# Alternating the two heads of a tile in the mixer's value matmuls

## The reference

```python
x = x + _L0_attn_ref(_L0_cond_ref(x, f, f, w, u, cond), W_in, conv_w, ...)
# in _L0_attn_ref:
def step(h, inp):
    dA_t, dt_t, x_t, B_t, C_t = inp
    u = (dt_t[:, :, None] * x_t)[..., None] * B_t[:, :, None, :]
    h = dA_t[:, :, None, None] * h + u
    y = jnp.einsum('bhpn,bhn->bhp', h, C_t)
    return (h, y)
y = moveaxis(ys) + D_param[None, None, :, None] * xs
g = y * _silu(gate)
g = g * rsqrt(mean(g * g) + EPS) * norm_w
return jnp.einsum('bli,di->bld', g, W_out)
```

## Time and profile before

| | us |
|---|---|
| median of 3 runs | 1449.42 |
| lowest and highest run | 1442.3, 1452.4 |
| span of the profiled execution | 1444.4 |
| PE busy | 1208.4 (84%) |
| PE weight loads busy | 641.6 (44%) |
| DVE busy | 879.5 (61%) |
| ACT busy | 593.9 (41%) |
| POOL busy | 569.6 (39%) |
| L655 MATMUL py, 512 records, busy | 71.1 |
| DVE's y (L935) waiting for PE's py (L655) | 49.7 in 20 waits |

### The profile page before, as it was taken

How to read it: one execution, slowest core, us unless ns; L and a number is a source line. 1 busy time by engine, 2 the same in 40 slices (tenths; PEclk the granted TensorE clock), 3 DMA queues, 4 the chain that set the end, 5 groups by cost and what they waited for, 6 DMA issues and landing times. The chain is left out here.

```text
span 1444.4 us, 16409 instructions
## 1 busy us (share of the span) xinstructions
PE 1208.4 (84%) x4614; PEld 641.6 (44%) x4614; DVE 879.5 (61%) x1244; ACT 593.9 (41%) x1742; POOL 569.6 (39%) x531
## 2 busy tenths in 40 slices
PE   0048899779897699999986898988799787997998
PEld 0014444334453344444434555643485336844443
DVE  7978999389985564246325948729741496504222
ACT  2025454454454232232224546647672476711110
POOL 5562675626665231002002856727651275500000
PEclk9999999999999799999998999989899898997999
DMA  6000000000003400000003000030000000000000
GB/s 253 0 22 1 0 1 1 1 0 0 0 0 120 157 0 1 0 0 0 33 10 136 1 1 0 0 138 1 1 2 1 1 0 0 0 0 8 0 0 29
DMA packets 5481, 33.24 MB, mean 23 GB/s; under 512 B 528, under 2 KB 1936, under 8 KB 3536
## 3 DMA queue, kind: packets, MB, share of 16 engines
q1 hardware_dynamic: 5424, 32.61, 5.8%
HBM read 31.56 MB, written 1.05 MB: 23 GB/s over the span
## 5 line engine op out<-in xcount | busy, mean ns | idle before, releaser
L813 POOL TENSOR_TENSOR decays<-decays,scores 128x768 f32<-128x768 f32 x64 | 124.8, 1953 | 152.0 <-ACT decays L749 152.0
L575 PE MATMUL pg<-h,weights 128*128 (+1 forms) x136 | 66.5, 612 | 85.5 <-PEq L356 82.6
L1998 POOL TENSOR_TENSOR f_pair<-m,weights 128x256 f32<-128x256 f32 x80 | 90.9, 1156 | 92.6 <-DVE m L2019 91.6
L1101 PE MATMUL ph<-h,weights 128*128 x256 | 116.5, 600 | 0.0
L1406 POOL TENSOR_TENSOR prob_latent<-prob_latent,inverse_latent 128x128 f32<-128x128 f32 (+1 forms) x128 | 81.5, 660 | 70.4 <-DVE inverse_latent L1396 70.1
L575 PE MATMUL px<-h,weights 128*128 x136 | 73.3, 664 | 26.1 <-DVE conv L886 26.0
L749 ACT ACTIVATE decays<-pcum,neg_cum 128x256 f32<-128x256 f32 (+1 forms) x256 | 87.7, 449 | 11.4 <-PE pcum L628 11.2
L1246 DVE TENSOR_TENSOR mid<-up,ph 128x512 f32<-128x512 f32 x44 | 30.2, 687 | 98.5 <-ACT up L1158 98.5
L1406 POOL TENSOR_TENSOR prob_gqa<-prob_gqa,inverse_gqa 128x128 f32<-128x128 f32 (+1 forms) x128 | 62.0, 506 | 58.4 <-DVE inverse_gqa L1396 56.8
L1158 ACT ACTIVATE up<-ph 128x512 f32<-128x512 f32 x44 | 26.3, 597 | 140.4 <-PE ph L1101 140.4
L886 DVE SCALAR_TENSOR_TENSOR conv<-px,pp,conv 128x510 f32<-128x510 f32 (+2 forms) x102 | 75.1, 737 | 14.5 <-ACT conv L714 11.6
(11 more groups left out here) (327 smaller groups left out, 3069.6 us busy)
## 6 DMA issues: line engine op xcount, KB each, us to landing
weights<-in_w_mixer SPq DMA_DIRECT2D x2, 2048.0 KB, 18.3
weights<-in_w_moe SPq DMA_DIRECT2D x2, 1536.0 KB, 7.8
moe_rest<-in_w_moe SPq DMA_DIRECT2D x2, 1536.0 KB, 13.9
weights<-in_w_gqa SPq DMA_DIRECT2D x1, 3072.0 KB, 10.2
weights<-in_w_gqa SPq DMA_DIRECT2D x1, 2048.0 KB, 14.7
weights<-in_w_moe SPq DMA_DIRECT2D x1, 1920.0 KB, 9.1
weights<-in_w_mixer SPq DMA_DIRECT2D x1, 1536.0 KB, 11.8
weights<-in_w_moe SPq DMA_DIRECT2D x1, 1152.0 KB, 11.7
```

What stands on the lines that cost most here:

```text
L575: op = nc.tensor.matmul(out[0:m, :], w[:, col + k * m:col + (k + 1) * m], net.h[:, ds(i * PAIR + k * TOK, TOK)], start=(k == 0), stop=(k = ...
L813: nc.gpsimd.tensor_tensor(decays[:, head % 4], decays[:, head % 4], scores[:], ALU.mult).then_inc(decay_scaled, 1)
L1101: op = nc.tensor.matmul(out[:], wt[:, n * D + k * P:n * D + (k + 1) * P], net.h[:, ds(i * PAIR + k * TOK, TOK)], start=(k == 0), stop=(k = ...
L1998: op = nc.gpsimd.tensor_tensor(out[:, :, s, :], src[:, :, 1 - s, :], sin[:, None, s, :].to_broadcast([P, 4, HALF]), ALU.mult)
```

## The change

In `mix`, the loop over the two heads of the tile goes from the outside to the inside. Before, the four matmuls of the first head stood ahead of the four of the second, with a wait for `decay_scaled` ahead of each head. Now each matmul of the first head is followed by the same one of the second head, and one wait for the scaled decays of both heads stands ahead of all.

```diff
-                for hh in range(TILE_HEADS):
-                    head = s * TILE_HEADS + hh
-                    pe.wait_ge(decay_scaled, i * HEADS + head + 1)
-                    rows = slice(hh * HEAD, (hh + 1) * HEAD)
-                    for b in range(BB):
-                        for r in range(ST):
-                            cols = slice(0, SEQ) if r == 0 else slice(SEQ, TRI)
+                pe.wait_ge(decay_scaled, i * HEADS + (s + 1) * TILE_HEADS)
+                for b in range(BB):
+                    for r in range(ST):
+                        cols = slice(0, SEQ) if r == 0 else slice(SEQ, TRI)
+                        for hh in range(TILE_HEADS):
+                            head = s * TILE_HEADS + hh
+                            rows = slice(hh * HEAD, (hh + 1) * HEAD)
                             op = nc.tensor.matmul(
                                 py[rows, b * SEQ + r * P:(b + 1) * SEQ],
                                 x_tok[:, s % 3, b * ST + r, rows],
```

## The result

The changed kernel takes 1438.08 us (median of 13 runs, 1431.1 to 1450.59) against 1447.5 us for the kernel before, timed beside it (median of 13, 1442.3 to 1459.14). The ratio is 0.9933 with a 95% interval of 0.991 to 0.9955, so 6.5 to 13.0 us less, 9.7 by the ratio.

A forecast was written before the change was run, and what follows sets the result against it. Steady steps were bound by PE and a nearly equal loop through POOL's pass and DVE's gate. Terms of 0.6, 1.88, 2.04 and 1.95 made 6.5 us a pair, 13.0 for both, less 0.5: 12.5 us, so 1437 us, range 1429 to 1447.

The forecast's parts named there:

- The mix: Value matmuls: head 2 starts 0.05 us behind head 1, a mix takes 1.57, saving 0.65 (bounds 0.56 and 0.70).
- Rival C: Value matmuls: alternating heads never run at once, a mix takes 2.9 us, 17 us slower in all, 1466; chance 0.08.
- The wait costs nothing: Before the mix: waiting for both heads' scaled decays costs nothing, with 0.91 us to spare in the closest case.
- Mix 0: First mix of a pair: y's 2.33 us wait loses 0.65, g is freed, `xs` meets the pass; 0.6 counted.
- Mix 5, 1.88: Gate at 186.31 moves 0.65 earlier, ahead of POOL's pass, and takes 0.68 us: gain 1.88 us a pair.
- rival D: PE's longer waits drop its clock to 1.2 GHz, two or three times: 5 us back, 1442; 0.20 shared with another rival.
- Mix 11, 2.04: Gate at 244.03 moves ahead of POOL's pass and ends at 244.06 in place of 246.10: gain 2.04 us.
- Mixes 7 to 10: Steady steps: gate still behind POOL's pass absorbs the 0.65, PE idles for ACT's exponentials; nothing counted.
- The tie of -0.03: Steady steps: gate starts 0.62 us behind POOL and moves 0.65 earlier, so which goes first is open.
- rival B: Gate wins the tie at mix 8, 9 or 10, DVE 1.05 us earlier: 3 to 7 us more, 1430 to 1434; chance 0.20.
- The tail, 1.95: Mixes 13 to 15, where the mix is on the only chain: 3 x 0.65 = 1.95 us a pair.
- the signs named in advance: Mix 1.5 to 1.65 us, y waits about 37, gates near 186 and 244 about 0.7, mixer 12 to 13 shorter.

The follow-up runs named there:

- the kernel by batch: Against the changed kernel: for each batch the two matmuls of head 1, then the two of head 2; 1430.03 us (one run).
- second execution of before: The kernel before, unchanged, timed and profiled once more; 1454.08 us, beside 1448.17 in the run next to it.
- the kernel with the clock kept up there: Changed kernel plus two matmuls adding zeros behind mix 4 of each pair, nowhere else; 1446.1 us (one run).
- the two kernels that kept the clock up there: Changed kernel plus zero-adding matmuls: two a pair behind mix 4 only, 1446.1 us; ten a pair in PE's long waits, 1436.28 us.
- the short pass: Changed kernel with POOL's scaling cut from 768 to 16 columns, so the output differs; 1408.49 us (one run), 1421.38 for the kernel before cut likewise.
- tail filled: Changed kernel with DVE's gate ahead of `take_x`, plus one zero-adding matmul behind mix 14; 1425.43 us (4 runs), ratio to before 0.9833.
- filled in all places: Changed kernel plus ten zero-adding matmuls a pair, after mixes 1, 4, 6, 12, 14 and 15; 1436.28 us (4 runs), ratio 0.9895.

## Why the prediction was right and wrong

The time is 1438.08 us where I gave 1437, inside 1429 to 1447, and within 1% of before. A good part of that is luck: the sum behind it was 12.5 us on the profiled execution, which shows 7.9, of which 6.2 can belong to the change (5.5 in the mixer and the 0.69 ahead of its first y). On the medians it is 9.7 of 12.4, and the median of three that the forecast started from was itself 1.9 above the later one of 13.

**The mix.** Right, and at the bound: head 2 starts 7 ns behind head 1, so the saving is 0.70 where I took 0.65, and PE's busy time of the line fell by 21.1 us for 20.8. Rival C is ruled out. My reason for giving it little, that the middle stretch of the earlier trace rows already runs the two heads at double pace, fits what was measured. The rule of the Trainium skill (TensorE: Matmul & The Clock Gate, Part 3, "The mechanism") on a strict order of starts, which I set against the trace, fails again: in the kernel by batch head 2 starts ahead of three older records. On the other hand the same page of the Trainium skill, in "Measured speedup vs the span model", gives about 4 ns for each further tile that runs beside the first; the 7 ns and the 1.52 us here are near it. Had I taken that figure of the page, the bound 0.70 would have been the middle value.

**The wait costs nothing.** Right. The kernel with only the wait has the mixer of the second execution of before to 0.2 us.

**Mix 0.** Right: y waits 1.64 for 2.33 us, a gain of 0.69 for 0.6, and as said the g behind it (0.69 for 2.20) was freed and `xs` was held instead. The rows of the kernel after, for this part and the next three:

```profile
127.70 0.75 DVE L935 SCALAR_TENSOR_TENSOR y<-xs,pp,py 128x512 f32<-128x512 f32 x1 [1.64 <-PE py L655]
...
129.09 2.31 DVE L895 SCALAR_TENSOR_TENSOR xs<-tanh_x,conv 128x512 f32<-128x512 f32 x1
...
183.68 1.82 POOL L813 TENSOR_TENSOR decays<-decays,scores 128x768 f32<-128x768 f32 x1 [3.51 <-ACT decays L749]
...
184.21 1.84 DVE L901 SCALAR_TENSOR_TENSOR gate<-tanh_g,gate 128x512 f32<-128x512 f32 x1
...
223.00 0.68 DVE L901 SCALAR_TENSOR_TENSOR gate<-tanh_g,gate 128x512 f32<-128x512 f32 x1
...
223.07 2.30 POOL L813 TENSOR_TENSOR decays<-decays,scores 128x768 f32<-128x768 f32 x1 [3.86 <-ACT decays L749]
...
229.53 0.75 DVE L935 SCALAR_TENSOR_TENSOR y<-xs,pp,py 128x512 f32<-128x512 f32 x1 [2.04 <-PE py L655]
...
230.46 2.22 POOL L813 TENSOR_TENSOR decays<-decays,scores 128x768 f32<-128x768 f32 x1 [2.09 <-ACT decays L749]
...
230.92 2.30 DVE L895 SCALAR_TENSOR_TENSOR xs<-tanh_x,conv 128x512 f32<-128x512 f32 x1
...
241.53 0.68 DVE L901 SCALAR_TENSOR_TENSOR gate<-tanh_g,gate 128x512 f32<-128x512 f32 x1
```

**Mix 5, 1.88.** Failed. The gate of its step begins at 184.21, still 0.53 behind the pass, and takes 1.84. The step that failed is "y has a wait of over 0.65 ahead of it, so the gate moves": it took PE's next projections as they were, but the longer wait behind mix 4 let the clock fall, px ended 1.1 us late, and y came no sooner. This is rival D at the place that it named, and the kernel with the clock kept up there shows the cause: the gate took 0.68. What neither the step nor the rival had was that the freed gate would start the slow rhythm, as it did in the two kernels that kept the clock up there.

**Mix 11, 2.04.** Mostly right. Its gate takes 0.68 (241.53) for 2.07, and y12 comes 1.77 us sooner relative to y7; the 0.65 of it that belongs to the mix arrives at y8, and 0.31 is lost at y11.

**Mixes 7 to 10.** Nothing was counted, and y8 to y11 together gained 0.4 us of 2.6: 0.70 at y8, and 0.31 lost at y11. So the main claim, that the 0.65 is absorbed here, stands for the sum. By the rows, DVE, ACT and PE's `pcum` close the loop as named up to y10; the 0.31 at y11 is lost to `xs` in the gate's place. The tie of -0.03 went to the gate at mix 9 by 0.07 us (223.00 against 223.07), which is rival B. It was to gain 1.05 and more; it gained nothing, because the next y then waited 2.04 us for PE and `xs` fell 0.46 behind the next pass and took 2.30. The wait of PE for ACT's exponentials set that step: its second projection began 2.99 us behind the first in place of 2.37. Rival B's price was read off the gate alone. The prediction had this very exchange at mix 0 and didn't carry it over to the steady step. By the Trainium skill (SBUF — State Buffer, "Who interferes with whom") a VectorE instruction with two SBUF inputs and a GpSimd instruction that reads SBUF exclude each other, and the one issued first goes first. The rows agree both ways: `xs` ends 0.54 behind the pass that was first, and the pass at 223.07, 0.07 behind the gate, takes 2.30 in place of 1.81. With one POOL pass in each DVE step, freeing one instruction moves the collision to another.

**The tail, 1.95.** Two of three. y13 and y14 gained 0.93 and 0.70; y15 lost 1.26. The term took the path of mix 15 as it was but for the mix, and two things changed on it. g was held for 0.30 us by the sum of squares, as the exchange at mix 0 could have told; and the wait of PE of 1.87 for 1.57 us was followed by a fall: 0.81 on the projection and 0.84 on the mix, together 1.65. The other kernels bear both out: y15 takes 5.01 us with g at 0.69 and the clock up (the short pass), 5.31 with g at 0.99 (tail filled), 6.02 with g at 1.70 (filled in all places). Rival D priced one fall at 1.66 and had it hidden nearly everywhere; here, on the only chain, it is not hidden, and I hadn't looked there. I had only looked for waits near 3 us.

**The yardstick.** The kernel before was read from one execution, and that showed its better rhythm, without a fall of the clock in mixes 4 to 12. Against this one the change is worth 5.5 us in the mixer, against the other execution 13.5 (355.1 - 341.6), and the 9.7 of the medians lies between. The changed kernel had the same mixer in both of its executions. So part of what the medians show may be that the slow rhythm was not seen in them any more, and this the prediction had not at all; how many of the timed runs had it isn't known. Its span was also set against the median of three, "5.0 below"; a run's time is 1.8 over its span, and the rest lies within the spread of the runs.

**Of the signs named in advance,** the mix, the first start of head 2, the gate near 244 and, on average, the steady period (9.02 for y8 to y11) came as said, and the later stages are unchanged (0.3 us). PE's new idle time ahead of `pcum` is 0.26 and 0.38 us in the steps at 222.53 and 241.45, with more of it inside the group: in the first of these the gate's projection began 0.62 us later behind px than before, which is the 0.6 named. The gates of mixes 8 to 10, named at 1.7 or more, took 2.21, 0.68 and 1.16. The waits of y (37 named, 44.1), the gate near 186 and the mixer (12 to 13 named, 5.5 to 6.2) did not come as said. In the chances, 0.20 and 0.13 for faster make 0.33 where 0.32 stands.

**Open.** How often the kernel before falls into the slow rhythm: two executions in three that ran its order with nothing added did, the kernel with one wait among them, but the timed runs don't show their inside. Why the clock fell behind mixes 4 and 6 in one execution of before and not in the other isn't settled either: the waits ahead of the two projections near 172 are alike, 2.40 and 2.41 us, with one at 2.96 us and the other at 1.98. Over all kernels with the mix of 2.22 and the late gate, such a wait ahead of this projection was followed by a fall in two of eight cases, and the 3.06 to 3.12 us of the shorter mix in six of six. Nor was it tried whether alternation by batch is really better than by matmul.

## What to carry to other kernels

Two 64-column matmuls on different halves of the array ran wholly side by side when they were issued in turn, and it cost a loop's place; blocks of up to four records were short enough here. But price a saving on the engine that then waits: look for each of its longer waits at what the clock does behind it, above all where it is on the only chain, and where two engines exclude each other count the next instruction that will be hit, not only the one that gets free. And look at a second execution of the kernel before, ahead of any sum over ties of a tenth of a microsecond.

## What the runs showed of the hardware

- A record of the second column half started ahead of three older records of the first that waited (8 starts in 0.70 us by batch), but not ahead of seven: there it started with the fifth record, after 0.71 us, with three waiting.
- Weight loads of both halves lay beside matmuls: 0.52 us of loads in 0.70 us with 0.66 of matmuls.
- A wait of PE of 2.41 us was followed by a projection at 2.4 GHz, one of 2.40 by a fall to 1.2 GHz, and one of 1.87 ahead of the last output projection as well, where one of 1.82 (by batch) had none. The length of the wait alone does not decide.
- A delay of PE by a few microseconds, once in a pair, changed the period of a pipeline of PE, DVE, ACT and POOL from 9.1 to 10.1 us for the three steps y9 to y11, with PE's granted clock at 1.00 throughout.
- DVE's instructions with two operands in SBUF were held by POOL's sum of squares as by its scaling: g took 0.69, 0.99 or 1.70 us at the same place of the pipeline, for POOL's pass out of its way, begun 0.82 us and begun 0.13 us ahead of it.
